# The calls of five engines in a new order: a quantised product with routed low-rank experts on one core

## The chip, the core and the metric

The kernel runs on one core of one Trainium2 chip. The core has a matrix engine (PE), a vector engine (DVE), an activation engine (ACT), a general engine (POOL) and a sequencer (SP) that here only issues transfers. Each engine runs its own list of instructions in the order written and waits on semaphores where it needs another engine. The metric is the device time of one execution, in microseconds, as the median of several runs.

## The reference

```python
# x: 2 x 1024 x 2048, ctx: 2 x 2048 x 2048, all float32; zero points 128
def fake_quant(x, scale, zp):
    q = clip(round(x / scale + zp), 0, 255)
    return (q - zp) * scale

x = x + tanh(g_xattn) * matmul(fake_quant(layernorm(x), x1_scale, x1_zp),
                               fake_quant(ctx, x2_scale, x2_zp))
y = layernorm(x)
logits = y @ route_w.T                       # 8 experts
weight = one_hot(argmax(logits), 8) * max(logits)
h = einsum('bsd,erd->bser', y, A)            # rank 16 per expert
out = x + tanh(g_ffn) * einsum('bser,eor->bso', weight[..., None] * h, Bw)
```

## The kernel before

**Tiles.** The 2 x 1024 rows of x are 16 tiles `t` of 128 rows, 0 to 7 of the first batch, 8 to 15 of the second. The context of a batch is cut into four column blocks `nb` of 512, each in four pieces of 1 MB; `ctx(0)` to `ctx(15)` belong to the first batch, `ctx(16)` to `ctx(31)` to the second. The product of one tile with one block is a unit of 16 matmuls, written as four runs `main(t, nb, run)` of four matmuls; run r needs piece r of its block.

**The path of a context piece.** SP loads it (`load_ctx`, L386), ACT quantises it to int8 (`affine_ctx`, L735), POOL (or ACT, L741) widens it to bf16 in `q2` (`widen_ctx`, L593). A piece of the second batch can be widened only when tile 7 is through with the block that it replaces.

**The path of a tile.** `load_x(t)` (L377); on DVE `stats1(t)` (L971, L973: mean and variance); on POOL `first_norm(t)` (L556 to L566); on ACT `affine_x(t)` (L753) to int8; on DVE or POOL the widening to bf16 (`widen_x`, and `widen_first(half)`, L1012, for the two halves of tile 0). Tiles 0 to 7 are transposed on PE (`turn_q1(t, half)`, L1503) and copied out by DVE (`take_q1T(t, half)`, L1021); later tiles by a transposing transfer (`flip_q1`, L416). After each unit DVE adds the product to the tile (`add_main`, L1104 and L1113). Then the second norm (`stats2_sum`, `second_norm`), y and its transpose (tiles 0, 1 and 15 on PE: `turn_y`, with `high_part` on ACT, L769, and `low_part` on DVE; the others through `norm_high`, `norm_full` on ACT, `low_rows` on POOL and `flip_high`, `flip_low` on SP), the products with A and the router (`h_group`, or `h_rows_high` and `h_rows_low`, L1613 to L1617, 48 short matmuls a tile), the expert's choice (`gate(t)`, L1155 to L1178, on DVE), `turn_wh` and `take_wh`, and the four products of a tile with the expert's weights, `expert_product(t, g)` (L1658 to L1660, three matmuls each), which DVE adds (`add_experts`, L1184) or, for tiles 13 and 14, ACT and POOL (`scale_part`, L835, and `add_part`). `store(t)` writes the tile out.

**Where things wait for room.** Units 0 to 11 rotate through four PSUM banks, later ones through two, `main0` and `main1`: a unit starts when the unit before it in its bank is added. `expert_product` alternates between two banks as well. Tiles share five homes in `xs` and three in `c8`: tile 6 takes the home of tile 0, 7 that of 2, 8 that of 3, 9 that of 4. So `load_x(9)` waits on SP until the store of tile 4 has landed, and everything that stands behind it on SP waits too.

**What sets the order.** Nothing but the text: behind the helpers each engine has a list of calls, one to a line (SP from L427, POOL from L616, ACT from L838, DVE from L1230, PE from L1669 on). `If` blocks such as `see_q1`, `unit_terms`, `tile_terms` and `column_sums` are passed over with these zero points.

Of the kernel before, what the change touches and what calls it, by code (L numbers as in the profile page):

```python
# [15 lines left out]
NB = D // NW  # L16
# [44 lines left out]
def build(nc, x, ctx, g_x, g_f, x1_scale, x1_zp, x2_scale, x2_zp, route_w, A, Bw, out):  # L61
# [13 lines left out]
    with st:  # L75
# [288 lines left out]
        def _(sp):  # L364
# [85 lines left out]
            load_b()  # L450
            load_ctx(16)
            load_ctx(17)
            load_ctx(18)
            load_x(5)
            load_ctx(19)
            load_ctx(20)
            load_ctx(21)
            load_ctx(22)
            load_ctx(23)
            load_ctx(24)  # L460
            flip_high(2)
            flip_low(2)
            store(0)
            flip_high(3)
            flip_low(3)
            load_x(6)
            load_ctx(25)
            store(1)
            flip_high(4)
            flip_low(4)  # L470
            store(2)
            load_ctx(26)
            load_x(7)
            load_ctx(27)
            flip_high(5)
            store(3)
            flip_low(5)
# [10 lines left out]
            flip_high(7)  # L488
            flip_low(7)
# [4 lines left out]
            load_x(12)  # L494
            flip_high(8)
            flip_low(8)
            flip_q1(10)
            flip_high(9)
            store(6)
            flip_low(9)  # L500
            flip_q1(11)
            store(7)
            flip_high(10)
            flip_low(10)
            flip_q1(12)
            load_x(13)
            load_x(14)
            flip_high(11)
            flip_low(11)
            flip_q1(13)  # L510
            store(8)
            flip_high(12)
            load_x(15)
# [3 lines left out]
            flip_high(13)  # L517
            flip_low(13)
            flip_q1(15)
            flip_high(14)  # L520
            flip_low(14)
            store(10)
# [13 lines left out]
        def _(pool):  # L536
# [81 lines left out]
            widen_ctx(0)  # L618
            widen_ctx(1)
            first_norm(2)  # L620
            widen_ctx(2)
            widen_ctx(3)
            widen_ctx(4)
# [3 lines left out]
            first_norm(3)  # L627
# [4 lines left out]
            first_norm(4)  # L632
# [4 lines left out]
            widen_x(4)  # L637
            second_norm(0)
            second_norm(1)
            second_norm(2)  # L640
            first_norm(5)
            second_norm(3)
            low_rows(2)
            widen_x(5)
# [1479 lines left out]
```

## Time and profile before

| what | us |
|---|---|
| median of three runs | 364.12 |
| lowest and highest run | 363.27, 364.35 |
| span of the profiled execution, first to last instruction | 361.7 |
| PE busy | 333.0 (92%) |
| DVE busy | 260.6 (72%) |
| ACT busy | 197.4 (55%) |
| POOL busy | 172.3 (48%) |
| DMA engines' mean rate | 242 GB/s |

The profiled execution has its span, 361.7 us, and no separate device time beside it; the median is 2.4 us above the span. "Busy" of an engine is the time in which at least one of its instructions was running. A matmul of 512 columns is shown with about 380 ns, since it includes the way through the array, while a new one starts every 216 ns; so the share of PE says how often it had something in it, not how full it was.

### The profile page before, as it was taken

To read this page: it belongs to the slowest core of one execution; us is meant where nothing else is said; L and a number is where in the kernel's file an instruction comes from. 1 tells how busy PE (TensorE), PEld (TensorE's weight loads), DVE (VectorE), ACT (ScalarE), POOL (GpSimd) and SP (SyncE) were. 2 spreads that over 40 slices of the span, in tenths; PEclk is the share of its full clock that TensorE was granted. 3 is DMA by queue.
4 is the path that set the end of the run, shared out by engine and by line. 5 is a ranking of instruction groups with operands and counts; after the bars stand their busy time and mean duration, and the time that the engine had idled before them with its cause. 6 is when DMAs were issued, how large, how long until landed. Compare 5 with 4: busy or idle time off the path is not lost.

```text
span 361.7 us, 5854 instructions
## 1 busy us (share of the span) xinstructions
PE 333.0 (92%) x2237; PEld 186.4 (52%) x2262; DVE 260.6 (72%) x553; ACT 197.4 (55%) x129; POOL 172.3 (48%) x199
## 2 busy tenths in 40 slices
PE   0389999999999999999998999999999999999983
PEld 0244454546756466455464546464464555465751
DVE  3855799898967896958658587945588567585853
ACT  1888489778967262747999270524062413204460
POOL 2559267431265162545999056627064441605281
PEclk9999999999999999999999999999999999999999
DMA  7999999895769998899799996666939890443956
GB/s 301 400 387 404 366 387 380 289 348 173 284 182 212 289 251 291 270 266 294 176 366 157 262 320 121 181 111 177 212 138 158 225 288 31 93 84 59 304 220 232
DMA packets 93906, 87.63 MB, mean 242 GB/s; under 512 B 71844, under 2 KB 72868, under 8 KB 89764
## 3 DMA queue, kind: packets, MB, share of 16 engines
q1 hardware_dynamic: 93856, 87.11, 79.5%
q8 instruction: 26, 0.43, 0.5%
q14 instruction: 12, 0.10, 0.1%
q10 hardware_dynamic: 12, 0.00, 0.0%
HBM read 52.49 MB, written 16.78 MB: 191 GB/s over the span
## 4 chain that ended last, share of the span: by engine, by line
PE 77%; DVE 8%; DMA 7%; issue 2%; ACT 2%; POOL 2%; ACTq 0%; SPq 0%; DVEq 0%
PE main L1575 46%; DMA xs<-in_x 4%; PE hp L1613 4%; PE hp L1617 4%; PE hp L1614 4%; PE outp L1575 4%; PE outp L1658 4%; PE outp L1660 3%; PE outp L1659 3%; DVE bn L971 3%; PE turn L1609 2%; DMA prow<-in_g_ffn 2%; DMA out<-xs 1%; ACT x L753 1%; PE turn L1503 1%
## 5 line engine op out<-in xcount | busy, mean ns | idle before, releaser
L1575 PE MATMUL main<-q,qa 128*128 128x512 bf16 x841 | 194.6, 380 | 5.0 <-POOL q L593 2.3
L1575 PEld LDWEIGHTS main<-q,qa 128*128 128x128 bf16 x864 | 83.2, 98 | 101.2 <-issue 2.7
L586 POOL TENSOR_TENSOR yn<-y,yn 128x2048 f16<-128x2048 f32 x13 | 53.0, 4077 | 31.7 <-ACT y L788 31.7
L735 ACT ACTIVATE c<-stage,zpc,inv 128x2048 int8<-128x2048 f32 x24 | 49.9, 2086 | 7.7 <-DMA stage<-in_ctx 4.0
L593 POOL CAST q<-c 128x2048 bf16<-128x2048 int8 x24 | 45.1, 1893 | 15.3 <-ACT c L735 14.8
L782 ACT ACTIVATE yn<-xs,sc 128x2048 f16<-128x2048 f32 x11 | 23.0, 2093 | 53.4 <-POOL sc L579 49.6
L1104 DVE SCALAR_TENSOR_TENSOR xs<-main,cc,xs 128x512 f32<-128x512 f32 x45 | 33.3, 740 | 21.7 <-PE main L1575 21.5
L574 POOL TENSOR_SCALAR ve<-mv 128x1 f32<-128x1 f32 x16 | 3.1, 191 | 84.8 <-DVE mv L1137 81.8
L1184 DVE SCALAR_TENSOR_TENSOR xs<-outp,tsc,xs 128x512 f32<-128x512 f32 x44 | 31.2, 735 | 13.6 <-PE outp L1660 13.5
L971 DVE BATCH_NORM_STATS2 bn<-xs 128x6 f32<-128x512 f32 x52 | 32.1, 680 | 10.6 <-DMA xs<-in_x 10.6
L753 ACT ACTIVATE x<-xs,sc 128x2048 int8<-128x2048 f32 x12 | 25.0, 2087 | 24.5 <-POOL sc L566 24.4
L1613 PE MATMUL hp<-WT,yT 128*128 128x136 f16 x256 | 34.9, 223 | 0.1
L1614 PE MATMUL hp<-WT,yT 128*128 128x136 f16 x256 | 34.9, 223 | 0.0
L1113 DVE BATCH_NORM_STATS2 bn<-xs 128x6 f32<-128x512 f32 x48 | 33.3, 694 | 1.7
L601 POOL CAST q<-x 128x2048 bf16<-128x2048 int8 x12 | 22.7, 1891 | 11.7 <-ACT x L753 10.0
L793 ACT ACTIVATE whT<-wp 128x256 f16<-128x256 f16 x16 | 6.0, 376 | 37.3 <-PE wp L1646 37.3
L1613 PEld LDWEIGHTS hp<-WT,yT 128*128 128x128 f16 x256 | 25.0, 98 | 2.4 <-DVE yT L1142 0.5
L1614 PEld LDWEIGHTS hp<-WT,yT 128*128 128x128 f16 x256 | 25.0, 98 | 1.7
L1658 PE MATMUL outp<-BT,whT 128*128 128x512 f16 x64 | 24.3, 380 | 0.7 <-ACT whT L793 0.5
L1660 PE MATMUL outp<-BT,whT 128*128 128x512 f16 x64 | 24.3, 379 | 0.0
L1659 PE MATMUL outp<-BT,whT 128*128 128x512 f16 x64 | 24.3, 379 | 0.0
L1617 PE MATMUL hp<-WT,yT 128*128 128x136 f16 x256 | 23.4, 223 | 0.0
(132 smaller groups left out, 435.2 us busy)
## 6 DMA issues: line engine op xcount, KB each, us to landing
stage<-in_ctx SPq DMA_DIRECT2D x24, 1024.0 KB, 7.9
xs<-in_x SPq DMA_DIRECT2D x13, 1024.0 KB, 6.5
out<-xs SPq DMA_DIRECT2D x12, 1024.0 KB, 5.0
yT<-in_ctx SPq DMA_DIRECT2D x4, 1024.0 KB, 9.2
y<-in_ctx SPq DMA_DIRECT2D x4, 1024.0 KB, 10.1
c<-in_x SPq DMA_DIRECT2D x3, 1024.0 KB, 7.4
out<-c SPq DMA_DIRECT2D x3, 1024.0 KB, 7.3
c<-in_L_ffn_A SPq DMA_DIRECT2D x1, 1024.0 KB, 11.5
```

The source lines that it names most:

```text
L586: pool.tensor_tensor(yn[:, 1, :], y[:, :], yn[:, 0, :], ALU.subtract).then_inc(s_ylo_made, 1)
L593: pool.tensor_copy(in_q2(piece), c8_of(piece)).then_inc(s_ctx_ready, 1)
L735: act.activation(c8_of(piece), place(piece), ACT.Identity, bias=zpc[:, 1:2], scale=inv[:, 1:2])\
L971: dve.bn_stats(bn1[:, t % 2, nb, :], xcol(t, nb * NW, (nb + 1) * NW)).then_inc(s_bn1_done, 1)
L1104: dve.scalar_tensor_tensor(out=xcol(t, c0, c1), in0=bank_of(n)[:, :], scalar=cc[:, :], in1=xcol(t, c0, c1), op0=ALU.mult, op1=ALU.add).the ...
L1575: last = pe.matmul(bank_of(n)[:, :], q1T(t)[:, k, :], q2[:, nb, k, :], start=(k == 0), stop=(k == KC - 1))
L1613: pe.matmul(hp[:, 0:WC], yT[:, 0, c, :], WT[:, c, 0:WC], start=(c == 0), stop=False)
L1614: pe.matmul(hp[:, 0:WC], yT[:, 0, c, :], WT[:, c, WC:2 * WC], start=False, stop=False)
L1617: return pe.matmul(hp[:, 0:WC], yT[:, 1, c, :], WT[:, c, 0:WC], start=False, stop=(c == KC - 1))
L1658: pe.matmul(o, whT[:, 0, :], BT[:, 0, g * NW:(g + 1) * NW], start=True, stop=False)
L1659: pe.matmul(o, whT[:, 0, :], BT[:, 1, g * NW:(g + 1) * NW], start=False, stop=False)
L1660: pe.matmul(o, whT[:, 1, :], BT[:, 0, g * NW:(g + 1) * NW], start=False, stop=True)\
```

## The change

Every call of the five lists is still there, once, with the same arguments; only the order of the lines differs, on all five engines. No helper, buffer, semaphore or constant is changed. Cut to the places at the start, around tiles 5 to 9 and at the end (SP first, then ACT, DVE and PE):

```diff
@@ -427,99 +427,99 @@
             load_x(0)
             load_x(1)
             load_ctx(0)
+            load_x(2)
             load_ctx(1)
-            load_x(2)
             load_ctx(2)
             load_ctx(3)
+            load_x(3)
             load_ctx(4)
             load_ctx(5)
+            load_router()
             load_ctx(6)
             load_ctx(7)
-            load_x(3)
             load_a()
-            load_router()
+            load_x(4)
             load_ctx(8)
-            load_x(4)
             load_ctx(9)
             load_ctx(10)
             load_ctx(11)
+            load_b()
             load_ctx(12)
...
             load_ctx(29)
+            store(4)
             flip_high(6)
+            load_x(9)
+            flip_q1(8)
             flip_low(6)
-            flip_q1(8)
-            store(4)
             load_ctx(30)
-            load_x(9)
             load_ctx(31)
...
@@ -835,126 +835,126 @@
...
+            take_wh(13)
             norm_group(15, 1)
-            take_wh(13)
-            norm_group(15, 3)
             scale_part(13, 0)
             scale_part(13, 1)
             high_part(15, 0)
             high_part(15, 1)
             scale_part(13, 2)
+            take_wh(14)
             scale_part(13, 3)
-            take_wh(14)
+            norm_group(15, 3)
             high_part(15, 2)
...
@@ -1229,95 +1229,94 @@
 
             widen_first(0)
             widen_first(1)
+            stats1(2)
             take_q1T(0, 0)
-            take_q1T(0, 1)
             see_q1(0)
             widen_x(1)
             see_q1(1)
-            stats1(2)
+            unit_terms(0, 0)
+            unit_terms(1, 0)
+            take_q1T(0, 1)
             take_q1T(1, 0)
...
@@ -1325,149 +1324,150 @@
             tile_terms(5)
             add_experts(1, 0)
             add_experts(1, 1)
+            stats1(6)
             take_q1T(5, 1)
+            gate(2)
...
             add_main(7, 0)
             add_main(7, 1)
...
+            stats1(9)
...
             add_main(7, 2)
             add_main(7, 3)
...
+            expert_product(12, 1)
             main(15, 0, 0)
...
-            expert_product(12, 1)
             expert_product(12, 2)
...
```

On DVE, at the start. The names: `x8` is tile 0 or 1 in int8, `q1` the same in bf16, `turn0` and `turn1` the PSUM banks of the two transposed halves, `qa` their home in SBUF, `xs` a tile of x, `bn1` its statistics. Before:

```order
L1012 CAST q1<-x8 128x1024 x2
L1021 COPY qa<-turn0 128x1024
L1021 COPY qa<-turn1 128x1024
L1070 COMPARE_AND_BRANCH
L1063 TENSOR_REDUCE rowc<-q1 128x1
L1065 TENSOR_SCALAR rowc<-rowc,cd,kdd 128x1
L1070 UNCONDITIONAL_BRANCH
L1007 CAST q1<-x8 128x2048
```

and now:

```order
L1012 CAST q1<-x8 128x1024 x2
L971 BN_STATS bn1<-xs 128x6 x4
L973 BN_AGGR mv1<-bn1 128x2
L1021 COPY qa<-turn0 128x1024
L1070 COMPARE_AND_BRANCH
L1063 TENSOR_REDUCE rowc<-q1 128x1
L1065 TENSOR_SCALAR rowc<-rowc,cd,kdd 128x1
L1070 UNCONDITIONAL_BRANCH
L1007 CAST q1<-x8 128x2048
```

The statistics of tile 2 stand ahead of the first copy of tile 0's transpose, and the copy of the second half has gone behind the cast of tile 1.

On SP, the first transfers; `yT`, `y` and `stage` are the places of the context pieces, `c8` that of tile 1 and of A. Before:

```order
L377 DMA c8<-in_x 128x2048
L386 DMA yT<-in_ctx_4096 128x4x512
L386 DMA y<-in_ctx_4096 128x4x512
L377 DMA xs<-in_x 128x2048
L386 DMA stage<-in_ctx_4096 128x4x512 x2
L386 DMA yT<-in_ctx_4096 128x4x512
L386 DMA y<-in_ctx_4096 128x4x512
L386 DMA stage<-in_ctx_4096 128x4x512 x2
L377 DMA xs<-in_x 128x2048
L390 DMA c8<-in_L0_ffn_A 128x2048
```

and now:

```order
L377 DMA c8<-in_x 128x2048
L386 DMA yT<-in_ctx_4096 128x4x512
L377 DMA xs<-in_x 128x2048
L386 DMA y<-in_ctx_4096 128x4x512
L386 DMA stage<-in_ctx_4096 128x4x512 x2
L377 DMA xs<-in_x 128x2048
L386 DMA yT<-in_ctx_4096 128x4x512
L386 DMA y<-in_ctx_4096 128x4x512
L393 DMA xs<-in_L0_ffn_route_w 8x2048
L386 DMA stage<-in_ctx_4096 128x4x512 x2
L390 DMA c8<-in_L0_ffn_A 128x2048
```

Tile 2 has moved from the fifth transfer to the fourth, tile 3 from the twelfth to the eighth; the context pieces from the fourth on come one place later, up to the place that tile 3 had.

On DVE, around the statistics of tile 9 (`main0` and `main1` hold units of tiles 7 and 8, `outp0` an expert product, `whs` the end of a `gate`, `bn2` the statistics after the product). Before:

```order
L1176 TENSOR_SCALAR whs<-hp,am 128x128
L1178 SCALAR_TENSOR_TENSOR whs<-hp,am,whs 128x128
L1184 SCALAR_TENSOR_TENSOR xs<-outp0,tsc,xs 128x512
L971 BN_STATS bn1<-xs 128x6 x4
L973 BN_AGGR mv1<-bn1 128x2
```

and now:

```order
L1104 SCALAR_TENSOR_TENSOR xs<-main0,cc,xs 128x512
L1113 BN_STATS bn2<-xs 128x6
L1104 SCALAR_TENSOR_TENSOR xs<-main1,cc,xs 128x512
L1113 BN_STATS bn2<-xs 128x6
L971 BN_STATS bn1<-xs 128x6 x4
L973 BN_AGGR mv1<-bn1 128x2
L1104 SCALAR_TENSOR_TENSOR xs<-main0,cc,xs 128x512
L1113 BN_STATS bn2<-xs 128x6
```

The statistics of tile 9 have moved ahead of the additions of tile 7's last two units; before, they stood behind the gate of tile 6 and the first expert addition of tile 5.

## Rows read from the trace of the kernel before

**Rows 1.** page, span and part 1: engine, busy us, share, instructions

```profile
span 361.7 us, 5854 instructions
...
PE 333.0 (92%) x2237; PEld 186.4 (52%) x2262; DVE 260.6 (72%) x553; ACT 197.4 (55%) x129; POOL 172.3 (48%) x199
```

**Rows 2.** windows: stretch, length, busy us of each engine, clock, DMA share, GB/s

```profile
14.40:30.00 15.60, 12.91 (x81) 7.58 (x83) 9.43 (x14) 13.57 (x8) 10.57 (x11) 1.00 1.05 388
...
70.00:110.00 40.00, 38.79 (x279) 23.35 (x281) 34.19 (x72) 32.36 (x24) 13.27 (x20) 1.00 0.71 235
110.00:190.00 80.00, 79.55 (x581) 45.30 (x586) 59.17 (x134) 51.22 (x31) 43.60 (x42) 1.00 0.92 270
190.00:200.00 10.00, 8.53 (x63) 4.76 (x63) 7.59 (x12) 9.70 (x6) 8.71 (x8) 1.00 0.88 161
200.00:336.10 136.10, 135.56 (x869) 73.20 (x876) 93.87 (x210) 44.71 (x28) 55.29 (x64) 1.00 0.66 162
```

**Rows 3.** waits of PE: what waited, for whom, us, times, longest

```profile
PE main L1575 <- POOL q L593: 2.3, 3, 1.1
```

**Rows 4.** timeline at the start: start, us, engine, line, operation

```profile
13.62 1.31 DVE L1012 CAST q<-x 128x1024 bf16<-128x1024 int8 x2 [0.64 <-DVE kdd L996]
...
14.47 1.86 PE L1503 MATMUL turn<-idb,q 128*128 128x128 bf16 x16 [5.70 <-DVE q L1012]
...
15.51 0.69 DVE L1021 COPY qa<-turn 128x1024 bf16<-128x1024 bf16 x1 [0.59 <-PE turn L1503]
...
16.95 1.86 PE L1575 MATMUL main<-q,qa 128*128 128x512 bf16 x4 [0.62 <-POOL q L593]
...
18.29 2.46 DVE L971 BATCH_NORM_STATS2 bn<-xs 128x6 f32<-128x512 f32 x4
...
21.11 2.55 PE L1575 MATMUL main<-q,qa 128*128 128x512 bf16 x11 [0.58 <-POOL q L593]
...
26.45 1.06 PE L1503 MATMUL turn<-idb,q 128*128 128x128 bf16 x16
```

**Rows 5.** DMA issues around 3 us: KB, us from issue to landing

```profile
y<-in_ctx SPq DMA_DIRECT2D x1, 1024.0 KB, 11.4
xs<-in_x SPq DMA_DIRECT2D x1, 1024.0 KB, 12.9
```

**Rows 6.** timeline of PE, last matmul of tile 0's fourth expert product

```profile
109.80 0.38 PE L1660 MATMUL outp<-BT,whT 128*128 128x512 f16 x1
```

**Rows 7.** timeline, tile 3 and the first product of block 2

```profile
36.20 2.47 DVE L971 BATCH_NORM_STATS2 bn<-xs 128x6 f32<-128x512 f32 x4 [0.44 <-DMA xs<-in_x]
...
40.70 2.09 ACT L753 ACTIVATE x<-xs,sc 128x2048 int8<-128x2048 f32 x1 [5.89 <-POOL sc L566]
...
44.16 1.07 PE L1503 MATMUL turn<-idb,q 128*128 128x128 bf16 x16 [0.60 <-DVE q L1007]
...
53.90 2.75 PE L1575 MATMUL main<-q,qa 128*128 128x512 bf16 x12
```

**Rows 8.** chain of waits, one whole unit of a tile

```profile
87.53 3.45 PE main L1575 x16
```

**Rows 9.** timeline, from tile 4's store to tile 9's statistics

```profile
178.66 0.36 SPq L405 DMA_DIRECT2D out<-xs  x1
...
187.45 5.59 SPq L421 DMA_TRANSPOSE yT<-yn  x1
...
190.24 2.48 DVE L971 BATCH_NORM_STATS2 bn<-xs 128x6 f32<-128x512 f32 x4 [2.39 <-DMA xs<-in_x]
...
193.87 2.76 PE L1575 MATMUL main<-q,qa 128*128 128x512 bf16 x11 [1.42 <-DVE xs L1104]
```

**Rows 10.** timeline of the end: last unit, y scaling on ACT, gate of tile 15

```profile
332.39 3.66 PE L1589 MATMUL main<-q,qa 128*128 128x256 bf16 x32
...
340.31 0.80 ACT L826 ACTIVATE y<-xs,sc 128x512 f32<-128x512 f32 x1
...
349.86 0.31 DVE L1155 TENSOR_TENSOR hp<-hp,wscale 128x136 f32<-128x136 f32 x1 [1.40 <-PE hp L1617]
```

More of the change, by code:

```diff
@@ L457, in _ @@
             load_ctx(21)
+            flip_high(2)
+            store(0)
+            flip_low(2)
+            load_x(6)
             load_ctx(22)
[L459 to L463, printed above, removed]
             flip_high(3)
             flip_low(3)
-            load_x(6)
-            load_ctx(25)
+            load_ctx(24)
+            load_ctx(23)
             store(1)
@@ L855, in _ @@
             affine_ctx(11)
-            mult_router()
+            permute_b()
+            affine_x(4)
             affine_ctx(12)
@@ L1313, in _ @@
             low_part(1, 3)
-            gate(1)
+            add_main(4, 1)
             add_experts(0, 0)
@@ L1318, in _ @@
             add_experts(0, 3)
-            add_main(4, 1)
-            gate(2)
+            gate(1)
             take_q1T(5, 0)
@@ L1342, in _ @@
             take_q1T(6, 0)
+            take_q1T(6, 1)
             stats2_sum(5)
-            tile_terms(6)
             add_experts(3, 0)
-            take_q1T(6, 1)
-            stats1(7)
             add_experts(3, 1)
+            gate(4)
             add_experts(3, 2)
@@ L1351, in _ @@
             add_main(6, 0)
+            stats1(7)
+            tile_terms(7)
+            add_experts(4, 0)
+            add_experts(4, 1)
             add_main(6, 1)
@@ L1701, in _ @@
+            main(1, 1, 2)
+            main(0, 1, 3)
+            main(3, 0, 1)
+            column_sums(3, [0])
+            main(1, 1, 3)
+            column_sums(3, [1])
+            column_sums(0, [2])
+            main(2, 1, 2)
+            main(3, 0, 2)
+            main(2, 1, 3)
+            main(3, 0, 3)
+            main(3, 1, 0)
             turn_a(0)
-            main(3, 0, 0)
-            main(3, 1, 0)
+            turn_a(1)
             main(3, 1, 1)
-            turn_a(1)
-            main(3, 0, 1)
@@ L1746, in _ @@
             main(1, 3, 0)
             main(1, 3, 1)
+            main(0, 3, 0)
+            main(3, 2, 3)
+            main(0, 3, 1)
+            column_sums(1, [3])
+            main(0, 3, 2)
             main(1, 3, 2)
+            main(0, 3, 3)
+            spread_scales()
             main(1, 3, 3)
@@ L1842, in _ @@
             main(6, 0, 0)
+            expert_product(3, 2)
+            main(6, 0, 1)
+            expert_product(3, 3)
+            main(6, 0, 2)
+            turn_wh(4)
+            main(6, 0, 3)
+            expert_product(4, 0)
+            expert_product(4, 1)
+            column_sums(7, range(NB))
+            main(6, 2, 0)
             main(6, 1, 0)
-            main(6, 0, 1)
             main(6, 1, 1)
-            expert_product(3, 2)
-            main(6, 0, 2)
-            expert_product(3, 3)
-            main(6, 0, 3)
             main(6, 1, 2)
-            turn_wh(4)
+            main(6, 2, 1)
             main(6, 1, 3)
-            main(6, 2, 0)
-            main(6, 2, 1)
+            main(6, 2, 2)
+            main(6, 2, 3)
             main(6, 3, 0)
             main(6, 3, 1)
-            main(6, 2, 2)
-            main(6, 2, 3)
             main(6, 3, 2)
@@ L1958, in _ @@
             main(10, 3, 3)
             h_rows_high(9)
+            main(11, 0, 0)
+            column_sums(11, range(NB))
+            expert_product(8, 1)
+            expert_product(8, 2)
             h_rows_low(9)
-            expert_product(8, 0)
-            column_sums(11, range(NB))
-            main(11, 0, 0)
+            expert_product(8, 3)
+            main(11, 0, 1)
+            main(11, 0, 2)
+            main(11, 0, 3)
             main(11, 1, 0)
-            main(11, 0, 1)
             main(11, 1, 1)
-            main(11, 0, 2)
+            turn_wh(9)
@@ L2040, in _ @@
             main(14, 1, 1)
-            main(14, 1, 2)
-            main(14, 1, 3)
+            expert_product(11, 0)
+            column_sums(14, range(NB))
+            expert_product(11, 1)
             main(14, 2, 0)
             main(14, 2, 1)
-            main(14, 3, 0)
-            main(14, 3, 1)
-            expert_product(11, 1)
+            main(14, 1, 2)
             main(14, 2, 2)
-            main(14, 2, 3)
-            main(14, 3, 2)
-            main(14, 3, 3)
+            main(14, 1, 3)
             expert_product(11, 2)
```

650 lines of the change are left out of this document (311 added, 339 removed).

## The prediction, made before the kernel was run

> **What bounds the kernel now.** I read the shares first, then the busy time by stretch, then PE's waits, then the timeline where PE waits, and last the order of the calls. PE is busy for 333.0 of 361.7 us [rows 1]. Before 14.4 us it has almost nothing, and after the last gate it waits on a chain. Between 110 and 190 us it misses 0.45 of 80 us and between 200 and 336 us 0.5 of 136 [rows 2]: there a new order can only lose. So PE is the bound, and what an order can give back are holes.
>
> Their size comes from the work. One matmul of 512 columns costs 3.45 / 16 = 0.2156 us [rows 8], a run of four 0.863, an expert product 0.647. 16 bf16 transposes issue in about 0.89 us, the 48 short matmuls of a tile in 2.85, four float transposes in 0.44 (estimates from the latencies and starts around [rows 4] and [rows 10]). Up to the fourth expert product of tile 0, at 109.80 + 0.22 = 110.0 us [rows 6], PE has issued 75 runs (64.7), five q transposes (4.5), those of A, B, the router and y (8.2), two tiles of short matmuls (5.7), four expert products (2.6) and small ones (0.5): 86.2 us. It starts at 14.5 [rows 4], so 95.5 have passed and **9.3 us are lost by then**. From there to the last unit of tile 15, near 336.05, about 2 us more are lost, 1.4 of them in one wait for an addition of DVE [rows 2, 9]. That is all there is to win, some 11 us, and much of it is bound by transfers.
>
> **The start.** At 13.62 DVE widens tile 0, at 15.51 it copies out its first transposed half, and the first product runs at 16.95, when the first context piece is ready [rows 4]. That ACT now makes half 1 before half 0 costs nothing: both are done by 12.7, and DVE comes only at 13.62. But the statistics of tile 2 (2.46 + 0.26, [rows 4]) now stand ahead of that copy. Their load is the fourth instead of the fifth; the fourth landed at 2.11 + 11.4 = 13.5, the fifth at 3.03 + 12.9 = 15.9 [rows 5], so DVE does not wait for it, and the copy ends near 18.4. The first product starts 1.5 us later. In return tile 2 has its norm near 19.3 instead of 22.8, its transposes are ready when PE comes, and the holes of before, while PE waits for pieces (2.3 us, [rows 3]), are filled with work already there. Placing the calls one behind the other with the durations of [rows 4], PE runs without a hole from about 22.0 and ends block 0 of tiles 0 to 2 near 32.7; before, that was 33.0. Net **-0.3**, between -0.3 and +1.5.
>
> The pace of PE belongs to this. In the first row of transposes 16 take 1.86 us, later 16 take 1.06, and four products take 1.86 [rows 4]: 116 ns for 128 columns is 1.2 GHz, while the granted clock reads 1.00 throughout [rows 2]; from 21.11 on products come at the pace of 2.4 GHz. If the rise comes later by the 1.5 us of the later start, half of that is lost; this is in the upper end. The Trainium skill ("TensorE: Matmul & The Clock Gate", Part 1) says that the number of slow matmuls at a kernel's start varies from run to run of the same kernel; by it this part could as well be nothing. The sum takes nothing.
>
> **Tile 3.** It was the twelfth load. DVE waited for it until 36.20, ACT quantised it at 40.70, and PE, with tiles 0 to 2 used up, waited for its transposes until 44.16 [rows 7]. As the eighth load it lands near 24.5 (2.7 us a load), its int8 form is ready near 34.6, and PE never runs dry. By my placement PE is through with blocks 0 and 1 of four tiles, A and the router near 53.7; before, the same work would end near 55.4 (53.9 at [rows 7], plus 1.5 for what stood behind). That is 1.4 beyond the start; I take **-1.1**, since each hand-over costs a little that a placement leaves out.
>
> **From 70 to 110.** PE misses 1.2 us there [rows 2], in waits on DVE's copies and additions, one engine's turn at a time. The new order puts four of B's copies between additions and two tiles' runs in alternation. The loads of pieces 12 to 15 come one place later, and B's load, now ahead of them, waits on SP for the last transpose of A, near 52.6, where the transfers run empty for some 2 us; the pieces are still 1.5 us early for PE. My placement finds no hole over 0.2 us up to 105, and is 4.2 us ahead of before there. Of the 2.5 beyond the terms above I take the visible **-1.2**; the range is 0 to -2.5.
>
> **Tile 6's statistics.** `stats1(6)` now stands ahead of `take_q1T(5, 1)`, which PE needs for the third run of tile 5. Its load waits for tile 0's store; a store and the load behind it took 190.24 - 178.66 = 11.6 us [rows 9]. I place the end of the statistics at 118.7 to 120.0 and PE's need at 120.2, and a gate right behind; **+0.6**, 0 to 1.2.
>
> **Tile 9's statistics.** Before, DVE waited for this load until 190.24 and PE 1.42 us for the addition behind it [rows 9]. Now `stats1(9)` stands ahead of the additions of tile 7's last two units, and `load_x(9)` behind `store(4)` and one transpose. From tile 4's last expert product PE has 16.3 us of work until `main(8, 0, 0)` needs the addition of unit (7, 2). DVE has 0.75 for the expert addition, 11.6 for store and load, 2.75 for the statistics, 0.75 for the addition, 15.9 in all, and hand-overs. So the old wait goes and about 0.5 takes its place: **-0.9**, between -1.4 and +1.7.
>
> **The last piece of the second context.** ACT now makes `affine_x(8)` behind its first widening, and eleven steps on context pieces and tile 9's quantising follow; at 1.9 to 2.1 us a step (as in [rows 7]) the last widening ends 0 to 0.9 us after PE wants it. **+0.5**, 0 to 0.9.
>
> **The end.** `expert_product(12, 1)` goes ahead of tile 15: 0.65 us of PE's work moves from behind the last unit to before it. Before, PE had 13.5 us of work from there to the end of tile 15's short matmuls and needed 13.8, so it ran nearly full; the gate follows at 349.86 [rows 10]. Now ACT scales the fourth group of y (0.80, [rows 10]) only after three expert scalings, and PE's last y transposes wait for it, near 10.4 us behind the last unit, where PE is free at 9.95. The rest of the chain is the same, so the stretch stays at 13.7 while 0.65 is added ahead: **+0.5**, 0 to 0.7. Behind the gate nothing is changed.
>
> **Sum.** -0.3 - 1.1 - 1.2 + 0.6 - 0.9 + 0.5 + 0.5 = -1.9 us. The span goes to 359.8, the time, 2.4 above it as before, to **362.2 us**.
>
> **Rivals.**
> (a) *The placement holds in full*: -4.2 up to 105 us, tile 6 and the last piece cost nothing, the 1.4 of tile 9 go, the end costs 0.5. -4.2 - 1.4 + 0.5 = -5.1, 359.0 us. For it: PE's holes there are real, 9.3 us. Against it: a placement has no hand-overs.
> (b) *The gain is given back*: the loads are the bound of the first 70 us, and PE, ahead by 2.6, waits in tiles 5 to 9 for the same stores, loads and norms. Only 0 to -1 stays, 363.7 us. For it: DVE is at 72% and the stretch to 190 had no hole to give.
> (c) *Slower: DVE stands behind a load*. Mechanism: `load_x(9)` waits on SP behind `flip_high(6)`, and issuing such a transpose took SP up to 5.59 us [rows 9]; with the short matmuls it needs ahead of it, the load goes out up to 2.6 later than the store allows. PE's cover is 16.3, DVE's need then 18.5: +2.2 on top of the 0.5. The same at tile 6 costs its full 1.2. With the last piece at 0.9 and the end at 0.7: -2.6 + 1.2 + (2.7 - 1.4) + 0.9 + 0.7 = +1.5, 365.6 us. It decides from where new waits of PE behind loads exceed 3.5 us in sum.
>
> That the change doesn't do what it says is no rival: the order of each engine is the text's.
>
> **How the numbers follow.** Forecast 0.40, (a) 0.15, (b) 0.20, (c) 0.25. A measurement of this kernel can tell about 0.3%, 1.1 us, from no change. The forecast and (a) are faster: 0.55; (b) within: 0.20; (c) slower: 0.25. The range takes in (a) with its end of -5.1 and (c) to a little over its price: 359.0 to 366.0. The forecast's own range is 360.6 to 363.0.
>
> **What would show it.** Right: the first product near 18.4; no wait of PE between 30 and 50 us; the fourth expert product of tile 0 done by 107.5; the wait for DVE around tile 8's first unit under 1 us; the gate of tile 15 at 13.7 us behind the last unit. Wrong: PE's first products slow beyond 24 us; DVE waiting over 3 us for a load of x at tile 6 or 9 with PE behind it; a hole in PE in tiles 10 to 15, which I did not place call by call.

## The result, and the profile after

| | before | after |
|---|---|---|
| median of 15 runs each | 363.54 | 365.36 |
| lowest and highest run | 363.11, 364.35 | 364.19, 367.06 |
| span of the profiled execution | 361.7 | 363.9 |

The changed kernel is 1.8 us slower: the ratio is 1.0047, with a 95% interval of 1.0032 to 1.0061. The forecast was 1.9 us faster, 362.2 us; the time lies inside the range, near the 365.6 of rival (c). The profiled execution of the changed kernel took 366.0 us, 0.6 above its median.

The page of the changed kernel, its shares and the chain that ended last:

```profile
PE 335.5 (92%) x2262; PEld 188.0 (52%) x2262; DVE 262.1 (72%) x553; ACT 197.2 (54%) x129; POOL 175.4 (48%) x199
...
PE 75%; DVE 10%; DMA 8%; SPq 3%; POOL 1%; issue 1%; ACTq 0%; DVEq 0%; ACT 0%
```

PE is as busy as before [rows 1], but the queue of SP, which issues the transfers, is now part of the chain (3%; before, 0%).

**The first 107 us went as forecast.** PE and DVE of the changed kernel at the start and at tile 0's fourth expert product:

```profile
18.37 1.89 PE L1575 MATMUL main<-q,qa 128*128 128x512 bf16 x4 [1.87 <-DVE qa L1021]
...
22.10 2.95 PE L1575 MATMUL main<-q,qa 128*128 128x512 bf16 x8
...
33.94 0.73 DVE L1104 SCALAR_TENSOR_TENSOR xs<-outp,cc,xs 128x512 f32<-128x512 f32 x1
...
106.21 0.38 PE L1660 MATMUL outp<-BT,whT 128*128 128x512 f16 x1
```

The fourth expert product ends at 106.4 instead of 110.0 [rows 6]; the new order has some work of other kinds left at that point, and at equal work PE is 2.3 us ahead. This trace is the low end: in the ten traces of kernels below that share its start and PE's order up to there, the same product ends at 104.9 to 106.1, which is 2.6 to 3.8 us ahead. Part of the difference is the rise of the clock at the start, told at the end.

**The loss is at tile 7.** SP, changed kernel: columns are start, time to issue, queue, line. L421 and L425 are transposing transfers, L405 a store, L386 a context load, L377 a load of x:

```profile
128.51 6.87 SPq L421 DMA_TRANSPOSE yT<-yn  x1
135.43 3.16 SPq L425 DMA_TRANSPOSE yT<-yn  x1
138.63 0.59 SPq L386 DMA_DIRECT2D stage<-in_ctx  x1
139.26 0.50 SPq L405 DMA_DIRECT2D out<-xs  x1
139.81 0.43 SPq L386 DMA_DIRECT2D stage<-in_ctx  x1
148.85 0.34 SPq L377 DMA_DIRECT2D xs<-in_x  x1
```

The same stretch of SP, kernel before:

```profile
129.89 2.09 SPq L421 DMA_TRANSPOSE yT<-yn  x1
132.49 1.82 SPq L425 DMA_TRANSPOSE yT<-yn  x1
136.90 0.34 SPq L405 DMA_DIRECT2D out<-xs  x1
137.29 0.52 SPq L386 DMA_DIRECT2D stage<-in_ctx  x1
141.85 0.34 SPq L377 DMA_DIRECT2D xs<-in_x  x1
```

`load_x(7)` waits for the landing of `store(2)`. That store took 4.9 us to land before and 9.6 after, and it went out 2.4 us later, behind a transposing transfer that held SP for 6.87 us instead of 2.09. So the load goes out 7.0 us later. DVE and PE of the changed kernel behind it:

```profile
155.42 2.47 DVE L971 BATCH_NORM_STATS2 bn<-xs 128x6 f32<-128x512 f32 x4 [5.57 <-DMA xs<-in_x]
...
159.57 0.74 DVE L1104 SCALAR_TENSOR_TENSOR xs<-main,cc,xs 128x512 f32<-128x512 f32 x1
...
160.37 5.31 PE L1575 MATMUL main<-q,qa 128*128 128x512 bf16 x16 [3.83 <-DVE xs L1104]
```

DVE stands for 5.57 us at `stats1(7)`, with two additions of tile 4 and the addition of unit (6, 1) behind it in its list; PE needs that last one for `main(6, 3, 0)` and waits 3.83 us. Its 16 products then take 5.31 us instead of the 3.45 of [rows 8]. The granted clock (the last but two column) says why:

```profile
160.00:162.00 2.00, 1.63 (x5) 0.67 (x6) 1.93 (x4) 2.00 (x1) 0.00 (x0) 0.70 1.03 359
162.00:164.00 2.00, 2.00 (x6) 0.76 (x5) 0.42 (x1) 0.57 (x2) 1.89 (x1) 0.50 1.19 308
```

It falls to 0.50, which is 1.2 of 2.4 GHz. (The column behind it, the share of the DMA engines, can read a little above 1.) Wait and slower products are 3.83 + 1.86 = 5.7 us.

**The balance.** -2.3 to 107 us, -1.4 for tile 9's old wait, which is gone, +5.7 at tile 7, +0.65 for the expert product moved ahead of tile 15: +2.65. This is a sum of what was seen, not exact: the last unit ends at 334.69 + 3.66 = 338.35 instead of 336.05, +2.3.

```profile
334.69 3.66 PE L1589 MATMUL main<-q,qa 128*128 128x256 bf16 x32
...
352.05 0.31 DVE L1155 TENSOR_TENSOR hp<-hp,wscale 128x136 f32<-128x136 f32 x1 [1.24 <-PE hp L1617]
```

The gate of tile 15 follows 13.7 us behind, as forecast.

**Why the transfers are late.** Two stretches of the kernel before (the last two columns are the share of the DMA engines and GB/s), and the same two of the changed kernel:

```profile
20.00:100.00 80.00, 75.60 (x471) 41.71 (x477) 65.99 (x113) 65.23 (x38) 38.29 (x46) 1.00 0.92 334
110.00:200.00 90.00, 88.08 (x642) 50.07 (x648) 66.76 (x146) 60.92 (x36) 52.31 (x49) 1.00 0.91 258
```

```profile
20.00:100.00 80.00, 79.32 (x499) 44.92 (x498) 67.33 (x112) 59.73 (x35) 40.76 (x39) 1.00 0.81 294
110.00:200.00 90.00, 85.97 (x598) 47.43 (x596) 63.94 (x143) 60.52 (x35) 48.99 (x50) 0.98 1.05 297
```

While PE got ahead, the transfers fell behind: 294 instead of 334 GB/s over 80 us are 3.2 MB. Before, SP had sent pieces 22 to 24 by 100 us; now `flip_high(2)`, `store(0)`, `flip_low(2)` and `load_x(6)` stand ahead of them, and ACT, which empties the buffers that they need, quantises piece 19 at 98.2 us where it had reached piece 22. These bytes are moved between 110 and 200 us, beside stores, loads of x and transposing transfers that wait for each other.

### The profile page after: what moved, and what is told of

Read it like the earlier page. It is cut to its first block, busy times and chain, and to the rows that moved or that the text cites. A ratio compares the mean times of both kernels' runs of the same rounds, so it can differ in the third digit from the quotient of the medians.

```text
span 363.9 us, 5880 instructions
## 1 busy us (share of the span) xinstructions
PE 335.5 (92%) x2262; PEld 188.0 (52%) x2262; DVE 262.1 (72%) x553; ACT 197.2 (54%) x129; POOL 175.4 (48%) x199
## 4 chain that ended last, share of the span: by engine, by line
PE 75%; DVE 10%; DMA 8%; SPq 3%; POOL 1%; issue 1%; ACTq 0%; DVEq 0%; ACT 0%
PE main L1575 46%; PE outp L1575 5%; PE hp L1617 4%; PE hp L1613 4%; PE hp L1614 4%; PE outp L1658 3%; PE outp L1660 3%; PE outp L1659 3%; DMA out<-xs 3%; SPq L421 2%; DVE bn L971 2%; DMA qa<-q 2%; DMA xs<-in_x 2%; DMA prow<-in_g_ffn 2%; PE turn L1609 1%; PE turn L1503 1%
## 5 line engine op out<-in xcount | busy, mean ns | idle before, releaser
L1575 PE MATMUL main<-q,qa 128*128 128x512 bf16 x864 | 202.2, 384 | 5.9 <-DVE xs L1104 3.8
```

Of the source, the lines that this page charges most:

```text
L1575: last = pe.matmul(bank_of(n)[:, :], q1T(t)[:, k, :], q2[:, nb, k, :], start=(k == 0), stop=(k == KC - 1))
```

## The experiments

Ratios are to the kernel before on the same chip, with 95% intervals. The medians of before lay between 363.5 and 363.9 us, so differences between kernels of different groups are taken from the ratios, times 363.6 us.

### First: which part of tile 7's chain

**e1_store_early** puts `store(2)` and `load_x(7)` ahead.

```diff
             flip_high(4)
+            store(2)
             flip_low(4)
+            load_x(7)
             load_ctx(26)
-            store(2)
             load_ctx(25)
-            load_x(7)
```

> The changed kernel with one edit on SP: from `flip_high(4)` on the list reads flip_high(4), store(2), flip_low(4), load_x(7), load_ctx(26), load_ctx(25) instead of flip_high(4), flip_low(4), load_ctx(26), store(2), load_ctx(25), load_x(7). Theory (the whole loss is tile 7's load, which came at 155.42 us because the store of tile 2 was issued at 139.26 and took 9.57 us to land beside two context loads): the store goes out near 135.4 and lands after 5 to 9.6 us, the load of tile 7 is issued at 140.4 to 145 and lands at 147 to 151.6; PE, which needs it by 151.6, does not wait before main(6, 3, 0), keeps its full clock, and the time falls by 4.6 to 5.7 us, to 359.7 to 360.8. Rival (the gain is given back anyway: another load, context pieces 25 and 26 for instance, becomes the wait): the time falls by 0 to 3 us, 362.4 to 365.4.

Measured: 364.76 us, 1.0033 (1.0015 to 1.0051). PE of this kernel:

```profile
142.51 1.12 PE L1617 MATMUL hp<-WT,yT 128*128 128x136 f16 x16 [2.07 <-DMA yT<-yn]
174.09 1.90 PE L1575 MATMUL main<-q,qa 128*128 128x512 bf16 x8 [0.43 <-DVE xs L1104]
185.57 2.75 PE L1575 MATMUL main<-q,qa 128*128 128x512 bf16 x12 [1.21 <-DMA qa<-q]
```

The wait of 3.83 us is gone and the clock stays up, yet three others come: for `flip_low(4)`, which now takes 5.17 us to issue instead of 3.16, for an addition, and for tile 8's transposing transfer. The profiled run took 363.6 us, the median of the twelve is 364.8: the trace shows a good case, and 1.2 us of its lead over the changed kernel's trace are there before tile 0's fourth expert product ends. The theory had the right place and took it for the whole loss; the rival had the size.

**e2_fill** hides 16 matmuls in PE's wait (`fill_turn(16)` ahead of `main(6, 3, 0)`), each `pe.matmul(turn[0][:, :], idb[:, :], q2[:, 3, k, :], ...)`.

> The changed kernel with 16 further matmuls of 512 columns on PE ahead of main(6, 3, 0), into a bank that nobody reads then (their result is not used). They take 3.45 us and lie in the 3.83 us for which PE waits there. Theory (PE's wait makes the granted clock fall, and this makes the 16 products behind it take 5.31 instead of 3.45 us): the products take about 3.5 us, the granted clock stays at 1.00, and the transposes of tile 7 start when its bf16 form is ready, at 163.99 instead of 165.52: 1.4 to 1.5 us faster than the changed kernel, about 363.9. Rival (the clock falls for another cause, load of the chip for instance): the same 5.31 us, no change, 365.4, or up to 366 if the fill is not fully hidden.

Measured: 365.07 us, 1.0040 (1.0026 to 1.0054). PE:

```profile
159.86 3.63 PE L1579 MATMUL main<-q,qa 128*128 128x512 bf16 x16 [0.73 <-DVE xs L1104]
187.03 2.75 PE L1579 MATMUL main<-q,qa 128*128 128x512 bf16 x12 [0.92 <-DMA qa<-q]
```

The 16 products run at full pace, so it was the idle time that cost the clock; but tile 8 is the next to be late, and of 1.5 us only 0.3 remain, which is within the noise.

**e3_stats7_later** moves `stats1(7)` behind `add_main(6, 1)` on DVE.

> The changed kernel with one edit on DVE: stats1(7) stands behind add_main(6, 1), no longer ahead of add_experts(4, 0), add_experts(4, 1) and add_main(6, 1). Theory (the late load is the cause, not its place on DVE): main(6, 3, 0) starts near 156.5 without a wait, but the statistics of tile 7 end near 159 instead of 157.9, its bf16 form is ready near 165.1, and PE waits some 5 us for it ahead of turn_q1(7, 0); the clock falls there instead. -0.4 us from the transposes, +0 to +1.9 from the slower work behind them: 365.0 to 367.0. Rival (the place on DVE is the cause: what stood behind the statistics is all that was late): the whole 5.7 us come back, 359.7.

Measured: 367.05 us, 1.0092 (1.0077 to 1.0108). PE:

```profile
164.26 1.89 PE L1503 MATMUL turn<-idb,q 128*128 128x128 bf16 x16 [4.86 <-POOL q L601]
```

PE waits 4.86 us for tile 7 itself: the place on DVE is not the cause, the load is.

**h1_new_start** joins the new start to the old rest.

> The new order of the changed kernel up to about 107 us, the order of before from there on: on each engine the first part of the new list and the rest of the old one, cut where both parts hold the same calls (SP behind load_ctx(21), POOL behind second_norm(1), ACT behind affine_ctx(16), DVE behind gate(1), PE behind h_group(1, 1)). Theory (the start brings 2.3 us that stay): 363.5 - 2.3 = 361.2 us, with tile 9's old wait of 1.4 us still there. Rival (gain given back: transfers bound the kernel, and PE, ahead of them, waits in tiles 5 to 9 for the same stores and loads): 363 to 363.8 us, with new waits of PE of 2 us in all between 110 and 200 us.

Measured: 379.79 us, 1.0467 (1.0436 to 1.0498). Both expectations missed. PE waited 7.67 us for y of tile 0: with the old list from `affine_ctx(17)` on, ACT has pieces 17 and 18 ahead of `norm_rows(0)`, whose loads the new start brings later. The cut lay in a place where the two orders are not interchangeable, and the run says nothing on the rest.

### Second: how much of it is bytes

**g1_light** and **m1_light8** keep the new order and cut the bytes of four and of eight context loads, **g2_before_light** and **m2_before_light8** do so in the old order:

```diff
+LIGHT = (22, 23, 24, 25)        # m1, m2: 22 to 29
...
+                if piece in LIGHT:
+                    sp.dma_start(place(piece).rearrange("p (c n) -> p c n", c=PK)[:, 0:1, :],
+                                 ctx_k[b, :, q * PK:q * PK + 1, nb * NW:(nb + 1) * NW]).then_inc(landed(piece)[0], 16)
+                    return
```

> The changed kernel, its order untouched, but the loads of context pieces 22 to 25 bring a quarter of their bytes (the other rows of these pieces are stale, so that part of the second context's product is not computed from the right data): 3 MB less to transfer between 110 and 150 us. Theory (transfers in debt: by 100 us the new order has loaded up to piece 21, the old one up to 24, about 3 MB of the 26.7 MB since 20 us; these fall into 110 to 200 us, where the transfers then run at a share of 1.05 and 297 GB/s against 0.91 and 258, so that stores, loads and transposes land late): store(2) lands in about 5 us instead of 9.57, stats1(7) starts by 151, PE does not wait before main(6, 3, 0), and the time falls by 5 to 6 us to 359.5 to 360.5. Rival (the order of calls is itself the cause, DVE and SP standing in a bad place): 364 to 365.4, the wait stays above 2 us.

> The kernel before with the same four loads cut to a quarter (again part of the product is not computed from the right data). Theory: it had no debt, its transfers had room between 110 and 200 us (share 0.91), so the light loads bring it little, 0 to 1.4 us (the one wait at tile 9), 362.1 to 363.6. Rival (any kernel of this kind gains by 3 MB less, so that the run of the changed kernel with light loads says nothing on its order): 358 to 360.

Measured: g1 364.30 us, 1.0000 (0.9980 to 1.0020); g2 363.39 us, 0.9983 (0.9971 to 0.9995). With 3 MB less the new order gains 1.7 us (1.0000 against 1.0047). The theory wanted 5 to 6; the time is in the range of the rival, by which the order of the calls is itself the cause, and the wait at tile 7 is just under the rival's 2 us:

```profile
157.47 2.76 PE L1580 MATMUL main<-q,qa 128*128 128x512 bf16 x11 [1.87 <-DVE xs L1109]
```

> The changed kernel, its order untouched, but the loads of context pieces 22 to 29 bring a quarter of their bytes (part of the second context's product is not computed from the right data): 6 MB less between 110 and 185 us, so that loads of x, stores and transposes meet no context load but 30 and 31. With pieces 22 to 25 alone (run g1_light) PE still waited 1.87 us at tile 7 and 1.10 for the transposed tile 8. Theory (the new order is sound for PE, and the transfers beside its stores and transposes take the gain): no wait over 0.5 us between 110 and 190 us, the first product of tile 8 near 182.0 instead of 187.66, time 359.5 to 360.5. Rival (the calls' own order holds SP or the engines up, without any contention): a wait of over 1 us at tile 7 or 8 stays, 362.5 to 364.3.

> The kernel before with the same eight loads cut to a quarter. Theory: its holes on PE behind 110 us are the 1.4 us at tile 9 alone, so 362.1 to 363.4, slower by 2 to 3 us than the changed order with the same light loads. Rival (the transfers hold both up alike): 360 to 361.

Measured: m1 **358.81 us, 0.9874 (0.9859 to 0.9888)**, below the theory's range; m2 363.54 us, 1.0000 (0.9991 to 1.0009). This pair decides between g1's theory and rival. The same stretch as above in m1, and how long the transfer that had held SP for 6.87 us takes to issue:

```profile
110.00:200.00 90.00, 89.58 (x616) 49.88 (x623) 67.90 (x149) 66.15 (x38) 48.95 (x49) 1.00 0.90 245
...
127.16 3.78 SPq L426 DMA_TRANSPOSE yT<-yn  x1
```

PE misses 0.42 of 90 us. The new order of calls is good for PE: with room in the transfers it is 4.7 us faster than the old order with the same bytes. (Between the two profiled spans, 363.9 and 356.6, 1.35 us lie ahead of tile 0's fourth expert product, where the two kernels are the same.) The old order gains 0.6 us at most from fewer bytes (g2), and none with 6 MB less (m2): its transfers were not what bound it. So what made the changed kernel slow is that it needs transfers in a stretch where they have no room.

**g3_before_late** does the harm to the old order: two loads behind 110 us, and on ACT `affine_ctx(23)` behind `take_wh(1)`. The edit on SP:

```diff
             load_ctx(22)
-            load_ctx(23)
-            load_ctx(24)
             flip_high(2)
             flip_low(2)
             store(0)
+            load_ctx(23)
             flip_high(3)
             flip_low(3)
             load_x(6)
+            load_ctx(24)
             load_ctx(25)
```

> The kernel before with load_ctx(23) behind store(0) and load_ctx(24) behind load_x(6) on SP (before, both stood ahead of flip_high(2) and went out by 100 us), and affine_ctx(23) behind take_wh(1) on ACT: 2 MB are moved from the stretch to 100 us, where the transfers have room, to the one behind 110. Theory (debt): the order of the units of PE and DVE is that of before, yet stores, loads and transposes between 120 and 160 us land 1 to 4 us later and the runs scatter as those of the changed kernel: +0.5 to +3 us, 364.1 to 366.6, a range over 2 us. Rival (only the new order of PE, DVE and SP behind 110 us matters): no change, 363.2 to 364.0.

Measured: 367.59 us, 1.0110 (1.0095 to 1.0124), four runs within 0.8 us of each other. SP and PE:

```profile
129.72 7.59 SPq L421 DMA_TRANSPOSE yT<-yn  x1
```

```profile
135.42 1.90 PE L1575 MATMUL main<-q,qa 128*128 128x512 bf16 x8 [1.84 <-DVE xs L1104]
139.64 0.22 PE L1613 MATMUL hp<-WT,yT 128*128 128x136 f16 x1 [1.34 <-DMA yT<-yn]
```

Moving 2 MB costs the old order 4.0 us, more than expected, and the same `flip_high(4)` takes 7.59 instead of 2.09 us to issue. The scatter that the theory foretold did not come. In this run ACT quantises pieces 24 and 25, and tile 6 behind them, some 6 us later too, so not all of the 4.0 are the transfers' crowding.

**f1_b_later** and **f2_pieces_early** try to win the bytes back by order alone. f1 puts `load_b()` behind `load_ctx(13)` and `affine_ctx(8)` ahead of `mult_a()`; f2 makes each of the pieces 17 to 22 one place earlier on ACT, and sends 22 and 23 earlier on SP:

```diff
             high_b()
+            affine_ctx(17)
             norm_rows(0)
...
+            load_ctx(22)
             flip_high(2)
             store(0)
             flip_low(2)
             load_x(6)
-            load_ctx(22)
+            load_ctx(23)
```

> The changed kernel with load_b() behind load_ctx(13) instead of ahead of load_ctx(12) on SP, and affine_ctx(8) ahead of mult_a() on ACT, which waits there from 39.4 to 45.66 us. Theory (debt): the hole in the transfers between 50 and 60 us (share 0.58, 197 GB/s) is filled by pieces 12 and 13, pieces 14 to 16 land 2 to 5 us earlier, but the next loads wait for ACT, which is the bound there, so 1 to 2 MB at most are gained by 100 us: -0.5 to -2 us, 363.4 to 364.9. Rival (only SP's order from 100 us on counts): no change, 365.0 to 365.8.

> The changed kernel with context pieces 17 to 22 one slot earlier on ACT (17 between high_b() and norm_rows(0), each later one where the piece before it stood, 22 right behind 21) and load_ctx(22) ahead of flip_high(2), load_ctx(23) ahead of flip_high(3) on SP. Theory (debt): 1 MB more is loaded by 101 us; a third to a half of the loss at tile 7 comes back, -1 to -3 us, 362.4 to 364.4. Rival (ACT has no room: the norms and halves of y of tiles 0 and 1 come up to 2 us later and PE waits for them in 80 to 105 us): 365.4 to 367.4.

Measured: f1 367.24 us, 1.0077 (1.0053 to 1.0101), above both expectations. PE waits 1.76 us for B and 4.28 us at tile 7, where the clock falls again, and between 20 and 100 us the transfers move no more than in the changed kernel (292 GB/s against 294). f2 364.58 us, 1.0013 (0.9992 to 1.0033): 1.2 us better than the changed kernel, just outside the theory's range, the wait at tile 7 down to 2.08.

### Third: can the gain be kept with all bytes

**k2_sp_only** puts each store and each load of x ahead of the transposing transfers beside it, **k1_stores_first** adds f2's idea, **k3_tuned** two more moves:

```diff
             flip_high(4)
+            store(2)
             flip_low(4)
+            load_x(7)
             load_ctx(26)
-            store(2)
             load_ctx(25)
-            load_x(7)
-            flip_high(5)
             store(3)
+            flip_high(5)
             load_ctx(27)
-            flip_low(5)
             load_x(8)
+            flip_low(5)
```

> The changed kernel with SP's list at tiles 4 and 5 as: flip_high(4), store(2), flip_low(4), load_x(7), load_ctx(26), load_ctx(25), store(3), flip_high(5), load_ctx(27), load_x(8), flip_low(5): each store ahead of the transpose whose issue would hold it up, each load of x ahead of the transpose behind it. In run e1_store_early, which did this for tile 7 alone, PE waited 2.07 us for flip_low(4) and 1.21 for flip_q1(8), which could go out only at 176.97 since load_x(8) was issued at 161.04. Theory: load_x(8) goes out near 157, flip_q1(8) near 175.8, the first product of tile 8 starts near 184.4 (187.66 in the changed kernel, 185.57 in e1_store_early); 362.0 to 363.0. Rival (the transfers are full there and whatever goes first pushes the others back): 363.5 to 365.

> k2_sp_only and in addition context pieces 17 to 22 one slot earlier on ACT (17 behind norm_rows(0)), load_ctx(22) ahead of flip_high(2) and load_ctx(23) ahead of flip_high(3) on SP. In run f2_pieces_early flip_high(4) took 4.22 instead of 6.87 us to issue. Theory: store(2) goes out near 133.5, flip_low(4) near 134, so that the wait of 2.07 us for it falls under 0.5, and tile 8's first product starts at 182.5 to 184.0: 360.5 to 362.0, the fastest of all. Rival (as for k2_sp_only): 363.5 to 365.

> k1_stores_first with two edits on SP: flip_low(4) ahead of store(2) again (in k1 PE waited 1.38 us for it; the load of tile 7 had room), and load_ctx(29), which ACT wants only near 183 us, behind flip_high(6) instead of ahead of store(4), so that less is under way when flip_high(6), which took 6.90 us to issue, and flip_q1(8), for which PE waited 1.79 us, go out. Theory (transfers in each other's way are what is left): the first wait falls under 0.4, the second under 1.0, the span of a run falls from 360.0 by 1 to 2.5 us; 360.8 to 362.5 us, faster than the kernel before. Rival: what is freed at one place comes back at the next, or tile 9 or piece 29 becomes late: 363 to 364.5.

Measured: k2 365.10 us, 1.0037 (1.0013 to 1.0061); k1 363.32 us, 0.9993 (0.9971 to 1.0015); k3 364.53 us, 1.0025 (1.0008 to 1.0042). k1 is the best order with all bytes, and not measurably better than before. PE in k1:

```profile
141.07 1.12 PE L1617 MATMUL hp<-WT,yT 128*128 128x136 f16 x16 [1.38 <-DMA yT<-yn]
183.93 2.75 PE L1575 MATMUL main<-q,qa 128*128 128x512 bf16 x12 [1.79 <-DMA qa<-q]
```

Its profiled run, 361.8 us, is near its lowest (361.4 to 365.3): these traces show the good case. The runs of k2 reach from 361.8 to 366.8, those of before from 362.9 to 364.6 in the whole study, but for one of 365.5.

### Fourth: the prediction's terms one by one

**s1_stats2_back** and **s2_end_old** start from m1_light8: `stats1(2)` behind `see_q1(1)`; the end as before.

> m1_light8 (358.8 us; its times scatter little, so a small term shows) with stats1(2) on DVE behind see_q1(1), no longer ahead of take_q1T(0, 0). The prediction's term for the start: the statistics ahead of the copy cost nothing and bring 0.3 us, so undoing them makes it 0.3 slower, 359.1, with the first product near 17.0 instead of 18.4 and a hole of up to 2 us later, before tile 2. Rival (the later first product costs as much as it starts later): 357.3 to 358.3.

> m1_light8 with the end as in the kernel before: expert_product(12, 1) behind the last unit of tile 15, ACT's list from norm_group(15, 1) on, PE's behind the last unit and DVE's behind stats2_sum(15) as before. The prediction's term for the end: the new order costs 0.5 us (0 to 0.7), so 358.1 to 358.8, likeliest 358.3. Rival (the end does not care): 358.8.

Measured: s1 363.01 us, 0.9983 (0.9972 to 0.9993); s2 358.48 us, 0.9856 (0.9840 to 0.9871). s1 loses 4.0 us against m1, and both its expectations missed. Its PE:

```profile
22.09 1.04 PE L1508 MATMUL turn<-idb,q 128*128 128x128 bf16 x8 [2.28 <-DVE qa L1026]
24.77 3.37 PE L1580 MATMUL main<-q,qa 128*128 128x512 bf16 x8 [1.65 <-POOL q L598]
```

The first product comes at 17.1, 1.2 us earlier, and then PE waits 3.9 us for what DVE and POOL do behind the later statistics. The eight products behind take 3.37 us; the same eight took 1.90 in m1. The new start hangs together: its one call that looks like a loss carries the rest. s2 gives back 0.3 us by the medians, 0.7 by the ratios; the intervals overlap, so the end's term of 0.5 fits but is not shown by it.

**b1_stats9_later** and **b2_tile3_earlier** do the moves for tile 9 and tile 3 in the old order. b1 moves `stats1(9)` behind `add_main(8, 1)`; b2 adds:

```diff
             load_ctx(6)
+            load_x(3)
             load_ctx(7)
-            load_x(3)
...
             add_main(1, 0)
+            stats1(3)
```

> The kernel before with one call moved on DVE: stats1(9) behind add_main(8, 1) instead of ahead of add_main(8, 0). There DVE waited 2.39 us for the load of tile 9 with two finished units behind it, and PE 1.42 us for the first of them. Theory (the prediction's term for tile 9, taken alone: the load does not come earlier, but nothing that PE needs stands behind it): PE's wait goes, tile 9's statistics end some 1.5 us later, which its transposing transfer at 199.39 us has room for: -1.4 us, 362.2, and the transfers, untouched up to there, keep the runs within 1.5 us of each other. Rival (tile 9 is itself needed at once, and the wait moves to its first unit): 363.3 to 363.8.

> b1_stats9_later, and in addition load_x(3) one place earlier on SP, ahead of load_ctx(7), and stats1(3) on DVE behind add_main(1, 0) instead of behind the three additions. Theory (the prediction's term for tile 3, as far as one load's place gives it): tile 3 lands near 33.5 instead of 36.2 us, its int8 form is ready 1.5 us earlier, PE's waits of 0.60 and 0.43 us around 44 us go, piece 7 is 2.7 us later and still in time; since the transfers and their order behind 50 us are those of before, the gain stays: -0.8 to -1.1 beside b1's, 361.1 to 361.5. Rival (piece 7 becomes late for the last run of block 1, or the gain is given back by 110 us): 362.0 to 363.0.

Measured: b1 364.38 us, 1.0012 (1.0003 to 1.0021); b2 366.20 us, 1.0074 (1.0054 to 1.0094). Both missed. PE in b1:

```profile
197.59 0.39 PE L1658 MATMUL outp<-BT,whT 128*128 128x512 f16 x1 [1.61 <-DVE xs L1184]
```

The wait went from the unit to tile 5's expert product, whose addition stands behind the statistics too. In b2 the statistics of tile 3 ended at 36.9 instead of 39.0, but the widening behind them (DVE):

```profile
43.74 1.23 DVE L1007 CAST q<-x 128x2048 bf16<-128x2048 int8 x1 [2.01 <-ACT x L753]
```

It comes 0.9 us later than before. Tile 3's norm stands behind the widening of piece 7 on POOL, and the load of that piece was what had been put back:

```profile
38.06 1.89 POOL L593 CAST q<-c 128x2048 bf16<-128x2048 int8 x1 [3.44 <-ACT c L735]
```

One load earlier is another load later. These 0.9 us, and the wait of 1.61 us that b2 has in common with b1, are part of b2's 2.7; where the rest goes was not traced.

## Why the prediction was wrong

**Right.** The start: its term was -0.3; the third addition of block 0 begins at 33.94 instead of 34.29. In the ten other traces with the same start it begins at 32.8 to 33.8, so -0.3 is the least that the start brought. The first product at 18.4 (18.37), no wait of PE between 30 and 50 us, tile 0's expert products by 107.5: all came. The stretch to 107 us was forecast 2.6 us ahead and is 2.3 in this trace, 2.6 to 3.8 in the ten others: the placement's 4.2 was less far off than this trace alone shows. Tile 9's old wait is gone and none takes its place (-1.4 where -0.9 was said); DVE waits 4.54 us for that load at 183.68, with nothing behind it that PE needs at once. The end: 13.7 us and 0.65 ahead of it, as written.

**Sizes off, mechanism right or harmless.** Tile 3 and the start together were to bring the router's end to 53.7; it ends at 54.7 in the changed kernel and at 54.1 in m1_light8, whose order is the same (before at equal work: 55.4). The two terms together were to be -1.4 and were -0.7 here and -1.3 there. In m1_light8 the start alone had brought 1.5 (its third addition begins at 32.82), so tile 3 added nothing to that; in the changed kernel it was -0.35. The -1.1 was too much. Tile 6's statistics wait 1.84 us for their load and PE for nothing: 0 instead of +0.6. The last piece of the second context: no wait, 0 instead of +0.5. Without tile 7 the terms seen in the changed kernel add up to -2.3 - 1.4 + 0.65 = -3.05, between the forecast and rival (a). The span of m1_light8, 356.6, is 5.1 below the old one, as rival (a) has it, but it comes from a faster start (3.7 ahead at tile 0's fourth expert product) and 6 MB less: that it hits the number is luck.

**The step that failed** is a term that the sum put at nothing without a reason: tile 7's statistics. The prediction priced those of tiles 6 and 9 and said nothing of tile 7, though there too a load waits for a store and DVE's additions for the load. Its only price for a store and the load behind it was 11.6 us, from the old trace [rows 9]; at tile 7 of the changed kernel they took 155.42 - 139.26 = 16.2 us, and the store itself went out 2.4 us later. What it cost is +5.7 us. The mechanism is the one of rival (c), DVE standing behind a load that SP sends late, and its point of decision (new waits over 3.5 us) is passed by 3.83 alone; only its place was wrong, and the fall of the clock behind a wait, 1.86 us, was in no rival. That the total comes near rival (c)'s +1.5 is luck all the same: none of the waits of PE that it priced, at tile 6, at tile 9 and at the last piece, came.

**The deeper error** is that durations of transfers were carried over from the old trace while the change moved the transfers. The prediction said of [rows 2] that "there a new order can only lose" and meant PE; the column of the DMA share stood beside it. A count of bytes by stretch would have pointed to it: every load that passes from before 100 us to behind it comes into a stretch where the share is 0.91 already. g1, m1 and g3 show this from three sides; e3 rules out the place on DVE alone; e1 rules out that tile 7's order on SP is the whole.

**What stays open.** How much of the loss is crowding and how much is the order of stores and transposing transfers was not parted: 3 MB less bring 1.7 us, another 3 MB 4.6, and k1 brings back 2.0 us with all bytes by order alone. Why the runs of most new orders scatter over 3 to 5 us when those of m1 and g3, four each, and s1, ten, stay within 1.6, was not found. Part of it goes with the clock: of the changed kernel's 15 runs, the five with a mean granted clock of 0.984 or 0.985 have a median of 366.19 us, the ten with 0.991 to 0.993 one of 364.8; e2, whose nine runs have 0.994 to 1.00, scatters over 1.9. That is seen, not tested. An order that keeps the 4.7 us with all bytes was not found either.

## What to carry to other kernels

When an order of calls changes, write down for each stretch the bytes that it moves beside the time that it wins, and compare the share of the DMA engines in the stretch that receives them. Durations of transfers in an old trace hold only where the same things are under way beside them. A wait that is taken away is a gain only up to what is next behind it: here four repairs of one place (e1, e2, e3, b1) each brought up another wait within 30 us.

## What the runs showed of the hardware

- **A transposing transfer holds its queue for longer when others are under way.** The same `flip_high(4)` took 2.09 us to issue when the last load had been sent 9.0 us and a store 4.6 us before it (before), 3.78 behind two light loads and a store sent within 6 us (m1), 6.87 behind two full loads and a store (after), 7.59 behind three and a store, sent within 6.2 us (g3). Everything behind it on SP waits, stores included.
- **The landing of `store(2)` doubled**, 4.9 to 9.6 us, behind a context load and a transposing transfer sent less than 4 us ahead.
- **PE's idle time can cost more than itself.** After idle times of 1.84 (g3), 1.87 (g1) and 2.08 us (f2) the products behind ran at full pace; with those of 3.83 (after), 4.28 (f1) and 4.86 us (e3) the granted clock fell to half, which cost the changed kernel 1.9 us. Filling the wait with other matmuls (e2) kept it up.
- **The rise of the clock at the start varies between executions of the same instructions**: the eight products from 22.1 us on took 2.95 us in the changed kernel and 1.90 in m1_light8, whose start is identical; over all thirteen traces with this start they took 1.90 to 2.98. The Trainium skill ("TensorE: Matmul & The Clock Gate", Part 1) says that the number of slow matmuls varies from run to run; the two traces agree, with about 1 us between them.
